# Routing of the first mixture's tokens inside the first attention

## The chip, the cores and the metric

One core of a Trainium2 chip runs the whole program, one launch. The metric is the device time in microseconds; lower is better. TensorE does the matmuls, VectorE and ScalarE the elementwise work and the reads of PSUM, GpSimd elementwise work in SBUF and indirect DMAs, SyncE issues the other DMAs.

## The reference, cut to what matters

Four layers on x of 8 sequences x 512 tokens x 256, fp32. The change touches the first and the head of the second:

```python
x = x + attn0(layernorm(x))            # 16 heads of 16, rope, causal softmax
y = layernorm(x)
logits = y @ gate_w                    # 8 experts
top_w, top_idx = top_k(logits, 2)
top_w = softmax(top_w)
x = x + sum_e combine[:, e] * (gelu(y @ w1[e] + b1[e]) @ w2[e] + b2[e])
# then a second attention with an MLP, and a mixture of 64 + 2 small experts
```

## The kernel before, in words

`attention0_phase` is one block of five instruction streams. The order of its work is written out: `ORDER` has, for each step (one pair of heads, 8 steps a sequence), the units of `STEP` (line 158), each with the number of steps that it runs ahead. `qk` turns keys and queries of a pair, `a0` to `a2` are score tiles of which VectorE takes the maxima (`a_top`), `m` turns the queries with the negated maxima in them, `b0` to `b2` are the scores again, whose exponentials ScalarE takes, `v0` to `v3` the products with the values (in even steps), `h` and `o` bring heads out and normalise them (`o` in odd steps). `BETWEEN` (line 160) hangs further units behind these: `x` turns the next sequence's normed tokens (step 0), `p0` to `p3` project its four tiles (steps 1 and 2), `t` and `y` turn and project the attention of the sequence before and add it to `g.x` (step 2), `n` norms the next sequence (step 7). Every engine follows the same order. Nearly all units share a ring of three PSUM tiles of two banks: TensorE's unit waits until the one three places back has been taken.

GpSimd puts the rope on the projected keys and queries of the next sequence and splits them (`stack_tile`, line 207: 13 operations a tile on GpSimd, or on VectorE for two tiles of the first sequence). Units `qk` of the next sequence begin in step 5 and wait for all four tiles (`stacked`). Then it adds a bias to `g.x`. VectorE also takes the statistics of the input during sequence 0. SyncE writes zeros into the 34816 rows of `sorted_x` and `sorted_y` by copying a first piece.

`route0_phase` (line 714 on) is the next block, on four groups of 8 tiles: statistics and the first guess of 1/sqrt on VectorE, three Newton steps on GpSimd (`rsqrt_refine`, line 77), normalisation into `g.y`, turning, logits by experts in three products of high and low parts, turning back, the choice of the best two experts on VectorE (15 small dependent operations, `choose`), ranks by matmuls with a triangle of ones, the rows of `sorted_x` (`place`), and 64 indirect scatters of 128 rows each by GpSimd (line 792), for which it waits at the end. Behind the last ranks VectorE makes the map of slots to experts, SyncE loads the first expert's weights and VectorE and ScalarE split them. Then comes the experts' block.

Of the kernel before, what the change touches and what calls it, by code (L numbers as in the profile page):

```python
# [88 lines left out]
def attention0_phase(nc, g, t):  # L89

    W3 = 3 * D
    with ExitStack() as ctx:
# [6 lines left out]
        def sig(name, per_turn=0):  # L99
# [21 lines left out]
        straight = sb("straight", [P, 2, H0, DH0])  # L121
# [20 lines left out]

        w_raw = probs[0][:, :, :].rearrange("p j c -> p (j c)")[:, 0:KC * W3].rearrange("p (c n) -> p c n", c=KC)
# [30 lines left out]
        RINGED = [unit for unit in ORDER if unit[0] in ("qk", "a0", "a1", "a2", "b0", "b1", "b2", "x", "p", "t", "y")]  # L174
# [4 lines left out]
        CLEARED, SPLITS = 11, 11 + 4  # L179

        BATCHES = ((0, TB), (TB, 2 * TB), (2 * TB, NT))
        steps_of = lambda batch: 2 * (batch[1] - batch[0]) + 5
        PREPARED = steps_of(BATCHES[0]) + steps_of(BATCHES[1]) + TB // 2 * 13
# [9 lines left out]
        turn_step, stacked = sig("turn_step", 11 * TB), sig("stacked", 2 * TB)  # L193
# [8 lines left out]
        attT_done, attT_hi, attT_lo = sig("attT_done", KC), sig("attT_hi", KC), sig("attT_lo", KC)  # L202
        proj_done, proj_added = sig("proj_done", TB), sig("proj_added", TB)
# [3 lines left out]
        def stack_tile(engine, n, m, turned, straight, step, done, turn):  # L207

            pairs_of = lambda ap: ap.rearrange("p h (d two) -> p h d two", two=2)
            for q in range(2):  # L210
                for e in range(2):
                    engine.tensor_tensor(pairs_of(turned[:, q])[:, :, :, e], pairs_of(qk[:, n, q])[:, :, :, 1 - e],
                                         pairs_of(unrope[:, n, q:q + 1, :])[:, :, :, e].broadcast_to([P, H0, DH0 // 2]),
                                         ALU.mult).then_inc(step.sem, step.tick())
                engine.tensor_tensor(straight[:, q], qk[:, n, q], rope[:, n, q:q + 1, :].broadcast_to([P, H0, DH0]),
                                     ALU.mult).then_inc(step.sem, step.tick())
            engine.wait_ge(step.sem, step.at(step.n, turn))
            for at in (0, DH0):
# [66 lines left out]
        def _(pool):  # L285
# [33 lines left out]
            for s in range(1, B):  # L319
# [3 lines left out]
                if s == 1:  # L323
                    refine(2)
# [2282 lines left out]
```

## Time and profile before

| | us |
|---|---|
| median of 3 runs | 2749.5 (2744.93 to 2750.41) |
| the profiled execution | 2746.9 |
| its span | 2745.2 |
| first attention's loop | about 76 to 580 |
| routing block | 580 to 709 |

The span is what the trace covers, the execution's own time lies 1.7 us above it. Starts in the trace are counted from the span's begin.

### The profile page before, as it was taken

How to read it: one execution, taken by the hardware profiler on the slowest of the kernel's cores; microseconds unless marked ns; L12 is line 12 of the kernel's file. 1: busy time of each engine (PE TensorE's matmuls, PEld its weight loads, DVE VectorE, ACT ScalarE, POOL GpSimd, SP SyncE). 2: the span in 40 equal slices, each digit the busy share in tenths (PEclk: the TensorE clock that was granted, in tenths of full speed). 3: DMA queues.
4: the chain of work that ended last, by engine and by line, in shares of the span. 5: the costliest groups of instructions: out<-in, count | busy, mean ns of one | idle time of the engine just before them, and what ended most of it. 6: DMA issues, size and time to landing. Idle time of an engine off the chain costs nothing. (4 is left out here: it accounts for less than half of the span.)

```text
span 2745.2 us, 53741 instructions
## 1 busy us (share of the span) xinstructions
PE 2419.3 (88%) x20524; PEld 2156.7 (79%) x20524; DVE 1799.5 (66%) x3223; ACT 1342.6 (49%) x2061; POOL 824.5 (30%) x1226
## 2 busy tenths in 40 slices
PE   4999999953599999935788898789999999999999
PEld 3666666632599999924677787689999999999999
DVE  7666666664488888849998888267444454544544
ACT  1555555631377777633444453344454554545454
POOL 4555566317200000055677766410000000000000
PEclk7899999976799999967899999989999999999999
DMA  9995000003477677747656565144222222222222
GB/s 302 332 334 169 2 2 2 2 6 126 156 241 238 234 230 240 220 131 181 154 148 156 152 168 147 40 138 143 91 90 86 83 89 88 86 89 87 89 78 87
DMA packets 195374, 373.31 MB, mean 136 GB/s; under 512 B 28964, under 2 KB 105960, under 8 KB 194152
## 3 DMA queue, kind: packets, MB, share of 16 engines
q1 hardware_dynamic: 185816, 343.31, 40.7%
q0 software_dynamic: 9360, 27.27, 3.0%
q8 instruction: 134, 2.20, 0.3%
q14 instruction: 64, 0.52, 0.1%
HBM read 336.95 MB, written 100.66 MB: 159 GB/s over the span
## 5 line engine op out<-in xcount | busy, mean ns | idle before, releaser
L2314 DVE TENSOR_TENSOR e_h_lo<-e_h,e_h_hi 128x512 fp32r<-128x512 f32 x320 | 222.0, 694 | 300.2 <-ACT e_h_hi L2390 300.2
L2452 PE MATMUL e_h_ps<-e_yT_hi,e_w_hi 128*128 128x256 f32 x1280 | 362.9, 283 | 3.0 <-ACT e_h L2376 2.2
L2468 PE MATMUL e_y_ps<-e_w_hi,e_h_hi 128*128 128x256 f32 x1280 | 359.1, 281 | 2.4 <-DVE e_h_lo L2314 2.3
L2452 PE MATMUL e_h_ps<-e_yT_hi,e_w_lo 128*128 128x256 f32 x1280 | 358.7, 280 | 0.0
L2452 PE MATMUL e_h_ps<-e_yT_lo,e_w_hi 128*128 128x256 f32 x1280 | 358.7, 280 | 0.0
L2468 PE MATMUL e_y_ps<-e_w_lo,e_h_hi 128*128 128x256 f32 x1280 | 355.7, 278 | 0.0
L2468 PE MATMUL e_y_ps<-e_w_hi,e_h_lo 128*128 128x256 f32 x1280 | 355.7, 278 | 0.0
L2390 ACT ACTIVATE e_h_hi<-e_h 128x512 fp32r<-128x512 f32 x320 | 202.2, 632 | 276.7 <-DVE e_h L2309 220.5
L2376 ACT ACTIVATE e_h<-e_h_ps,e_b 128x512 f32<-128x512 f32 x320 | 218.9, 684 | 175.0 <-PE e_h_ps L2452 151.3
L2309 DVE TENSOR_TENSOR e_h<-e_h,e_spread 128x512 f32<-128x512 f32 x256 | 176.8, 691 | 133.5 <-ACT e_h L2376 132.4
L462 DVE TENSOR_REDUCE a_top<-a_ring 128x2 f32<-128x1024 f32 (+3 forms) x256 | 204.2, 819 | 72.2 <-PE a_ring L651 70.8
L2452 PEld LDWEIGHTS e_h_ps<-e_yT_hi,e_w_hi 128*128 128x128 f32 x1280 | 243.7, 190 | 4.8 <-ACT e_h L2376 2.6
L2468 PEld LDWEIGHTS e_y_ps<-e_w_hi,e_h_hi 128*128 128x128 f32 x1280 | 240.9, 188 | 3.9 <-DVE e_h_lo L2314 3.3
L2452 PEld LDWEIGHTS e_h_ps<-e_yT_lo,e_w_hi 128*128 128x128 f32 x1280 | 241.7, 189 | 0.0
L2452 PEld LDWEIGHTS e_h_ps<-e_yT_hi,e_w_lo 128*128 128x128 f32 x1280 | 241.6, 189 | 0.0
L2468 PEld LDWEIGHTS e_y_ps<-e_w_lo,e_h_hi 128*128 128x128 f32 x1280 | 240.9, 188 | 0.2
L2468 PEld LDWEIGHTS e_y_ps<-e_w_hi,e_h_lo 128*128 128x128 f32 x1280 | 240.4, 188 | 0.0
L79 POOL TENSOR_TENSOR e_by_tile<-e_by_tile 128x4 f32<-128x4 f32 x24 | 8.5, 356 | 746.3 <-DVE e_by_tile L71 745.1
L517 ACT ACTIVATE a_probs<-a_ring 128x1024 f32<-128x1024 f32 (+1 forms) x192 | 168.8, 881 | 98.3 <-PE a_ring L665 97.0
L1290 PE MATMUL e_y_ps<-e_w_hi,e_h_hi 128*128 128x256 f32 x624 | 179.0, 287 | 2.9 <-DVE e_h_lo L1180 2.3
L1276 PE MATMUL e_h_ps<-e_xT_hi,e_w_hi 128*128 128x256 f32 x624 | 174.4, 280 | 1.6 <-DVE e_xT_lo L1173 1.6
L1276 PE MATMUL e_h_ps<-e_xT_hi,e_w_lo 128*128 128x256 f32 x624 | 174.2, 279 | 0.0
(371 smaller groups left out, 6772.6 us busy)
## 6 DMA issues: line engine op xcount, KB each, us to landing
e_w<-in_w SPq DMA_DIRECT2D x78, 1024.0 KB, 5.6
e_spread<-share_store SPq DMA_DIRECT2D x512, 128.0 KB, 2.8
a_keys<-rows_store SPq DMA_DIRECT2D x128, 256.0 KB, 5.0
a_queries<-rows_store SPq DMA_DIRECT2D x86, 256.0 KB, 4.9
a_running_hidden<-rows_store SPq DMA_DIRECT2D x42, 256.0 KB, 4.7
e_xs<-sorted_x SPq DMA_DIRECT2D x39, 256.0 KB, 5.1
sorted_y<-e_ys POOLq DMA_DIRECT2D x39, 256.0 KB, 5.9
e_stage_buf<-in_w_all SPq DMA_DIRECT2D x10, 512.0 KB, 3.9
```

Source lines behind the costliest of these rows:

```text
L79: pool.tensor_tensor(tmp, guess, guess, ALU.mult).then_inc(step.sem, step.tick())
L462: dve.reduce_max(top[r % 2][:, tb, :], banks(k)[:, :, at:at + (tb + 1) * P], AX.X).then_inc(top_taken.sem, top_taken.tick())
L517: act.activation(probs_of(s, r)[:, :, B_AT[i]:B_AT[i] + B_WIDTH[i]], banks(k)[:, :, 0:B_WIDTH[i]], ACT.Exp).then_inc(probs_ready.sem, prob ...
L1276: last = pe.matmul(h_ps[:, at:at + SLOT_TOKENS], l, r, start=(m == 0), stop=(m == len(ops) - 1))
L1290: last = pe.matmul(y_ps[n][:, 0:D], h_parts[a][:, f, n * P:(n + 1) * P], w2_parts[k][w][:, f, :], start=(f == 0 and m == 0), stop=(f == FC ...
L2309: dve.tensor_tensor(h[:, q % 2, :], h[:, q % 2, :], spread[r % SPREADS][:, :], ALU.mult).then_inc(scaled.sem, scaled.tick())
L2314: dve.tensor_tensor(h_parts[q % 2][1][:, :], h[:, q % 2, :], h_parts[q % 2][0][:, :], ALU.subtract).then_inc(h_lo.sem, h_lo.tick())
L2376: act.activation(h[:, q % 2, :], h_ps[q % 2][:, :], ACT.Silu, bias=b1[:, c:c + 1]).then_inc(h_ready.sem, h_ready.tick())
L2390: act.activation(h_parts[q % 2][0][:, :], h[:, q % 2, :], ACT.Copy).then_inc(h_hi.sem, h_hi.tick())
L2452: last = pe.matmul(h_ps[q % 2][:, cols], l, r, start=(m == 0), stop=(m == len(ops) - 1))
L2468: last = pe.matmul(y_ps[n][:, 0:D], h_parts[q % 2][a][:, n * P:(n + 1) * P], w2[b][:, c, :], start=(q == 0 and m == 0), stop=(q == CH - 1 ...
```

## The change

- The routing of sequence q is a set of new units in the loop, one sequence behind: `S0` statistics (step 3), `S1` scale and first guess, `S2` Newton steps (step 4), `N` normalisation (step 5), `U` turning, `L` logits, `T` turning back and `C0` first choice (step 6), `C1` second choice, `K` ranks, `W` rows (step 7). `U`, `L`, `T` and `K` take places in the ring. The last sequence's run behind the loop.
- The Newton steps are 9 VectorE operations instead of 12 on GpSimd.
- The norm `n` of sequences 3 to 7 moves from step 7 to step 3.
- The choice takes 12 operations behind the copy instead of 15, the placing 5 instead of 8.
- `stack_tile` has 8 operations over the same elements instead of 13.
- GpSimd scatters sequence q behind the stack and bias of sequence q+2, and the last two behind the loop. The normalised tokens lie in the third and fourth tile of the projected keys and queries, so VectorE waits for the scatters before it writes the third.
- SyncE spreads zeros over `sorted_x` first, then over `sorted_y` in smaller pieces, one at a time. Three more small loads and six VectorE operations for the constants stand at the start.
- The routing block keeps the map, the shares and the first weights, with two small loads; GpSimd waits for the scatters there.

```diff
         STEP = (("a0", 2), ("b0", 0), ("v0", -1), ("m", 1), ("a1", 2), ("qk", 3), ("b1", 0), ("o", -2), ("v1", -1), ("a2", 2),
                 ("v2", -1), ("b2", 0), ("v3", -1), ("h", -1))
         BETWEEN = {("b1", 0): ("x",), ("b0", 1): ("p0",), ("b1", 1): ("p1",), ("b2", 1): ("p2",), ("b0", 2): ("p3",),
-                   ("b1", 2): ("t",), ("b2", 2): ("y",), ("a2", 1): ("n",)}
+                   ("b1", 2): ("t",), ("b2", 2): ("y",), ("a2", 1): ("n",), ("a2", 5): ("n",),
+                   ("b1", 3): ("S0",), ("b0", 4): ("S1",), ("b1", 4): ("S2",), ("b1", 5): ("N",), ("b0", 6): ("U",),
+                   ("b1", 6): ("L",), ("v2", 5): ("T",), ("b2", 6): ("C0",), ("b0", 7): ("C1",), ("b1", 7): ("K",),
+                   ("o", 5): ("W",)}
         ORDER = []
         for step in range(-3, B * PAIRS + 2):
             for what, ahead in STEP:
                 s_, r_ = divmod(step + ahead, PAIRS)
                 ORDER.append((what, s_, r_))
                 for extra in BETWEEN.get((what, r_), ()):
-                    of = s_ - 1 if extra in ("t", "y") else s_ + 1
+                    of = s_ - 1 if extra[0] in "tySNULTCKW" else s_ + 1
+                    if extra == "n":
+                        of = (s_ + 1 if s_ < 2 else B) if r_ == 1 else (s_ + 2 if s_ else B)
                     if 0 <= of < B:
                         ORDER.append((extra[0], of, int(extra[1:] or 0)))
 
...
-        def stack_tile(engine, n, m, turned, straight, step, done, turn):
...
+        def stack_tile(engine, n, m, turned, step, done, turn):
+
+            pairs_of = lambda ap: ap.rearrange("p q h (d two) -> p q h d two", two=2)
+            mix = unrope[:, n].rearrange("p q (d two) -> p q d two", two=2).unsqueeze(2)
+            for e in range(2):
+                engine.tensor_tensor(pairs_of(turned[:, :])[:, :, :, :, e], pairs_of(qk[:, n])[:, :, :, :, 1 - e],
+                                     mix[:, :, :, :, e].broadcast_to([P, 2, H0, DH0 // 2]), ALU.mult).then_inc(step.sem, step.tick())
             engine.wait_ge(step.sem, step.at(step.n, turn))
+            engine.tensor_tensor(qk[:, n], qk[:, n], rope[:, n].unsqueeze(2).broadcast_to([P, 2, H0, DH0]),
+                                 ALU.mult).then_inc(step.sem, step.tick())
+            engine.wait_ge(step.sem, step.at(step.n, turn))
+            twice = lambda ap: ap.unsqueeze(2).broadcast_to([P, H0, 2, DH0])
+            engine.tensor_tensor(q_stack[m][:, n, :, 0:2 * DH0].rearrange("p h (u d) -> p h u d", u=2), twice(qk[:, n, 0]),
+                                 twice(turned[:, 0]), ALU.add).then_inc(step.sem, step.tick())
+            engine.tensor_tensor(k_stack[m][:, n, :, 0:4 * DH0].rearrange("p h (u two d) -> p h u two d", u=2, two=2)[:, :, :, 0],
+                                 twice(qk[:, n, 1]), twice(turned[:, 1]), ALU.add).then_inc(step.sem, step.tick())
+            engine.wait_ge(step.sem, step.at(step.n, turn))
+            engine.tensor_tensor(qk[:, n], qk[:, n], turned[:, :], ALU.add).then_inc(step.sem, step.tick())
...
+            def spread(name, at, size, behind):
+                dst, src = (t[rows][a:a + size, :].rearrange("(p r) d -> p (r d)", p=P)
+                            for rows, a in ((name, at), ("sorted_y", 0)))
+                sp.dma_start(dst, src).then_inc(behind.sem, behind.tick(16))
+
+            END = BLOCKS * SLOT_TOKENS
+            for at in range(0, END, TOKENS):
+                spread("sorted_x", at, min(TOKENS, END - at), zeros_spread)
+            sp.wait_ge(zeros_spread.sem, zeros_spread.at(zeros_spread.n))
+            for at in range(TOKENS, END, TOKENS // 2):
+                spread("sorted_y", at, min(TOKENS // 2, END - at), spread_zeros)
+                sp.wait_ge(spread_zeros.sem, spread_zeros.at(spread_zeros.n))
...
+            def scatter(q):
+                if q == 0:
+                    pool.wait_ge(zeros_spread.sem, ZERO_SPREADS * 16)
+                pool.wait_ge(rows_ready.sem, rows_ready.at(1, q))
+                for k in range(2):
+                    for n in range(TB):
+                        row = q * TB + n
+                        pool.indirect_dma_start(
+                            out=t["sorted_x"][:, :], out_offset=bass.IndirectOffsetOnAxis(ap=g.row[k][:, row:row + 1], axis=0),
+                            in_=y[:, n, :], in_offset=None).then_inc(written.sem, 16)
+
             prepare()
             for s in range(1, B):
+                turn_step.n = stacked.n = 0
+                for n in range(TB):
+                    stack(s, s % 2, n)
                 turn_step.close()
                 add_bias(s)
                 if s == 1:
                     refine(2)
+                else:
+                    scatter(s - 2)
+            scatter(B - 2)
+            scatter(B - 1)
...
+            def row_statistics(q):
+                y_step.n = 0
+                dve.wait_ge(proj_added.sem, proj_added.at(TB, q))
+                for n in range(TB):
+                    dve.bn_stats(y_stats[:, n, :], g.x[:, q * TB + n, :]).then_inc(y_step.sem, y_step.tick())
+
+            def row_scale(q):
+                dve.wait_ge(y_step.sem, y_step.at(TB, q))
+                dve.tensor_copy(y_half[:, 0:1], y_stats[:, 0, 0:1]).then_inc(y_step.sem, y_step.tick())
+                for n in range(TB):
+                    dve.bn_aggr(y_mv[:, n, :], y_stats[:, n, :]).then_inc(y_step.sem, y_step.tick())
+                dve.wait_ge(y_step.sem, y_step.at(2 * TB + 1, q))
+                dve.tensor_scalar(y_var[:, :], y_mv[:, :, 1], EPS, None, ALU.add).then_inc(y_step.sem, y_step.tick())
+                dve.wait_ge(y_step.sem, y_step.at(2 * TB + 2, q))
+                dve.tensor_scalar(y_half[:, :], y_var[:, :], -0.5, None, ALU.mult).then_inc(y_step.sem, y_step.tick())
+                rsqrt_seed(dve, y_step, q, y_rstd[:, :], y_var[:, :])
+
+            def row_refine(q):
+                y_refined.n = 0
+                dve.wait_ge(y_step.sem, y_step.at(2 * TB + 5, q))
+                for i in range(3):
+                    dve.tensor_tensor(y_newton[:, :], y_rstd[:, :], y_rstd[:, :], ALU.mult).then_inc(y_refined.sem,
+                            y_refined.tick())
+                    dve.wait_ge(y_refined.sem, y_refined.at(3 * i + 1, q))
...
+            def normalise(q):
+                if q + 2 < B:
+                    dve.wait_ge(stacked.sem, stacked.at(2 * TB, q + 2))
+                if q:
+                    dve.wait_ge(written.sem, written.at(0, q))
+                for n in range(TB):
+                    dve.tensor_scalar(y[:, n, :], g.x[:, q * TB + n, :], y_mv[:, n, 0:1], y_rstd[:, n:n + 1],
+                                      ALU.subtract, ALU.mult).then_inc(y_ready.sem, y_ready.tick())
+
...
+            def choose(q, k):
+                current = (logits, masked)[k]
+                best = g.best[k][:, q * TB:(q + 1) * TB]
+                dve.tensor_reduce(best, current[:, :, :], AX.X, ALU.max).then_inc(route_step.sem, route_step.tick())
+                routed()
+                dve.tensor_tensor(A[:, :, :], current[:, :, :], wide(best), ALU.is_equal).then_inc(route_step.sem, route_step.tick())
+                routed()
+                dve.tensor_tensor(A[:, :, :], ids[:, :, :], A[:, :, :], ALU.mult).then_inc(route_step.sem, route_step.tick())
+                routed()
+                dve.tensor_reduce(first[:, :], A[:, :, :], AX.X, ALU.min).then_inc(route_step.sem, route_step.tick())
+                routed()
+                dve.tensor_tensor(pick[k][:, :, :], ids[:, :, :], wide(first[:, :]), ALU.is_equal).then_inc(route_step.sem,
+                        route_step.tick())
+                routed()
+                if k == 0:
+                    dve.scalar_tensor_tensor(out=masked[:, :, :], in0=pick[0][:, :, :], scalar=-HUGE, in1=logits[:, :, :],
+                                             op0=ALU.mult, op1=ALU.add).then_inc(route_step.sem, route_step.tick())
+                    routed()
+                else:
+                    dve.tensor_tensor(both[:, :, :], pick[0][:, :, :], pick[1][:, :, :], ALU.add).then_inc(picked.sem, picked.tick())
+
+            def place_rows(q, k):
+                dve.wait_ge(ranked.sem, ranked.at(1, q))
+                dve.tensor_tensor(rank[:, :, :], ring[k][:, 0:TB * E0].rearrange("p (n e) -> p n e", n=TB),
+                                  g.head[:, :].unsqueeze(1).broadcast_to([P, TB, E0]), ALU.add).then_inc(route_step.sem,
+                                          route_step.tick())
+                routed()
...
+                dve.tensor_tensor(placed[:, :, :, :], rank[:, :, :].unsqueeze(1).broadcast_to([P, 2, TB, E0]), picks[:, :, :, :],
+                                  ALU.mult).then_inc(route_step.sem, route_step.tick())
+                routed()
+                dve.tensor_reduce(row_f[:, :, :], placed[:, :, :, :], AX.X, ALU.add).then_inc(route_step.sem, route_step.tick())
+                routed()
+                dve.tensor_copy(g.rows[:, :, q * TB:(q + 1) * TB], row_f[:, :, :]).then_inc(rows_ready.sem, rows_ready.tick())
+                dve.wait_ge(rank_taken.sem, rank_taken.at(1, q))
...
+                    if r == 2 and s >= 3:
+                        dve.wait_ge(written.sem, written.at(0, s - 2))
                     biased(s, m, r, k)
...
+            def transpose_rows(q, k):
+                pe.wait_ge(y_ready.sem, y_ready.at(TB, q))
+                for c in range(KC):
+                    for n in range(TB):
+                        last = pe.transpose(ring[k][:, c * S + n * P:c * S + (n + 1) * P], y[:, n, c * P:(c + 1) * P], g.ident[:, :])
+                    last.then_inc(yT_done.sem, yT_done.tick())
+
+            def find_logits(q, k):
+                pe.wait_ge(yT_lo.sem, yT_lo.at(KC, q))
+                split_product(ring[k][0:E0, 0:S], [((gate_hi[:, c, :], gate_lo[:, c, :]), (xnT_hi[:, c, :], xnT_lo[:, c, :]))
+                                                   for c in range(KC)]).then_inc(gates_done.sem, gates_done.tick())
+
...
+            def find_ranks(q, k):
+                pe.wait_ge(picked.sem, picked.at(1, q))
+                ranks = ring[k][:, 0:TB * E0]
+                pe.matmul(ranks, tri[:, :], both[:, :, :].rearrange("p n e -> p (n e)"), start=True, stop=False)
...
+            transpose_rows(B - 1, 2)
+            find_logits(B - 1, 0)
+            turn_logits(B - 1, 1)
+            find_ranks(B - 1, 2)
...
         @block.gpsimd
         def _(pool):
...
+            pool.wait_ge(g.written.sem, g.written.at(0, B))
...
```

## Rows read from the trace of the kernel before

**Rows 1.** Busy time by stretch: us, then busy us of PE, PEld, DVE, ACT, POOL (instructions), clock, DMA.

```profile
76.50:580.40 503.90, 489.08 (x5483) 331.51 (x5481) 323.26 (x616) 285.17 (x371) 269.28 (x404) 0.99 0.33 110
580.40:709.20 128.80, 41.31 (x240) 25.44 (x240) 65.99 (x258) 15.68 (x26) 73.53 (x112) 0.60 0.24 84
```

**Rows 2.** Timeline of POOL: start, us taken, operation, count; in brackets the idle time before.

```profile
404.78 1.00 POOL L212 TENSOR_TENSOR a_turned<-a_qk,a_unrope 128x128 f32<-128x128 f32 x2 [25.20 <-DVE a_qk L393]
...
408.19 1.42 POOL L219 TENSOR_TENSOR a_q_stack<-a_straight,a_turned 128x256 fp32r<-128x256 f32 x2
...
441.01 2.79 POOL L302 TENSOR_TENSOR x<-x,a_bias_proj 128x256 f32<-128x256 f32 x4
```

**Rows 3.** Timelines of DVE and POOL from the attention's end to the experts' start.

```profile
579.66 0.75 DVE L428 TENSOR_TENSOR x<-x,a_ring 128x256 f32<-128x256 f32 x2 [0.60 <-PE a_ring L535]
...
580.78 0.09 DVE L894 MEMSET r_three_halves<- 128x32 f32 x1 [0.37 <-PEq L92]
...
672.47 0.96 POOL L792 DMA_INDIRECT sorted_x<-y,row  x1 [0.30 <-issue]
...
673.73 1.84 POOL L792 DMA_INDIRECT sorted_x<-y,row  x1 [0.30 <-issue]
...
700.97 0.96 POOL L792 DMA_INDIRECT sorted_x<-y,row  x1 [0.30 <-issue]
...
709.19 0.20 DVE L1167 MEMSET scratch<- 128x1 f32 x6 [32.12 <-PEq L712]
```

**Rows 4.** Timelines of DVE and ACT in the routing block.

```profile
581.27 2.36 DVE L813 BATCH_NORM_STATS2 r_stats<-x 128x6 f32<-128x256 f32 x7
...
656.25 0.23 DVE L844 COPY r_logits<-r_lg_ps 128x64 f32<-128x64 f32 x1 [5.46 <-PE r_lg_ps L1023]
...
662.97 0.19 DVE L922 TENSOR_TENSOR r_apart<-r_best 128x32 f32<-128x32 f32 x1
...
666.59 0.17 DVE L952 CAST slot_expert<-r_over 1x40 int32<-1x40 f32 x1
...
673.52 1.23 DVE L964 CAST e_w_hi<-e_w 128x2048 fp32r<-128x2048 f32 x1 [5.60 <-DMA e_w<-in_w]
...
678.00 1.91 ACT L991 ACTIVATE e_w_hi<-e_w 128x2048 fp32r<-128x2048 f32 x1 [14.57 <-DMA e_w<-in_w]
```

**Rows 5.** Timeline of PE: in the loop, the last row in the routing.

```profile
397.08 1.09 PE L542 MATMUL a_ring<-ident_f,a_xn 128*128 128x128 f32 x8
...
401.93 0.39 PE L535 MATMUL a_ring<-a_w_lo,a_xnT_hi 128*128 128x512 f32 x1
...
402.16 0.39 PE L535 MATMUL a_ring<-a_w_hi,a_xnT_lo 128*128 128x512 f32 x1
...
628.80 0.34 PE L1036 MATMUL r_rank_ps<-r_both,r_ones 128*128 128x8 bf16 x8
```

**Rows 6.** Busy time by stretch, steps 3, 4 and 5 of sequence 5.

```profile
426.77:432.44 5.67, 5.58 (x74) 3.99 (x76) 4.40 (x8) 4.14 (x6) 5.51 (x8) 1.00 0.00 0
432.44:439.38 6.94, 6.94 (x92) 3.85 (x92) 4.47 (x7) 4.61 (x6) 6.86 (x11) 1.00 0.01 2
439.38:444.83 5.45, 5.18 (x66) 3.73 (x64) 4.05 (x9) 4.08 (x6) 4.26 (x7) 1.00 0.02 5
```

**Rows 7.** Timelines of DVE and POOL, small operations beside the stack.

```profile
111.77 0.66 DVE L71 TENSOR_SCALAR a_rstd<-a_rstd 128x24 int32<-128x24 int32 x1
...
438.07 0.17 DVE L468 TENSOR_SCALAR a_q_stack<-a_top 128x8 fp32r<-128x8 f32 x1
...
438.13 1.29 POOL L224 TENSOR_TENSOR a_qk<-a_straight,a_turned 128x512 f32<-128x512 f32 x1
...
438.28 1.18 DVE L471 SCALAR_TENSOR_TENSOR a_q_stack<-a_top,a_q_stack 128x8 fp32r<-128x8 f32 x1
```

**Rows 8.** Timeline of PE and busy time by stretch, in sequence 0.

```profile
115.17 0.72 PE L637 MATMUL a_pT<-a_ident_r,a_q_stack 128*128 128x128 f32 x4 [1.35 <-DVE a_q_stack L471]
...
118.00:121.00 3.00, 3.00 (x23) 2.11 (x24) 0.83 (x4) 2.05 (x2) 2.61 (x8) 0.50 1.01 328
```

More of the change, by code:

```diff
@@ L266, in _ @@
                                 const_loaded.tick(16))
+            for dst, src in ((tri_raw, t["earlier"][:, :]), (gate_raw, t["gate0"].rearrange("(c p) e -> p c e", p=P)),
+                             (ids[:, :, :], t["expert_ids"][0:TB, :].partition_broadcast(P))):
+                sp.dma_start(dst, src).then_inc(const_loaded.sem, const_loaded.tick(16))
             load_x(2)
@@ L272, in _ @@
             for at in range(0, TOKENS, step):
-                sp.dma_start(t["sorted_x"][at:at + step, :].rearrange("(n p) d -> p n d", p=P), zeros).then_inc(zeroed.sem,
+                sp.dma_start(t["sorted_y"][at:at + step, :].rearrange("(n p) d -> p n d", p=P), zeros).then_inc(zeroed.sem,
                         zeroed.tick(16))
             sp.wait_ge(zeroed.sem, zeroed.at(zeroed.n))
-            for rows, start in (("sorted_x", TOKENS), ("sorted_y", 0)):
-                for at in range(start, BLOCKS * SLOT_TOKENS, TOKENS):
-                    size = min(TOKENS, BLOCKS * SLOT_TOKENS - at)
-                    dst, src = (t[name][a:a + size, :].rearrange("(p r) d -> p (r d)", p=P)
-                                for name, a in ((rows, at), ("sorted_x", 0)))
-                    sp.dma_start(dst, src).then_inc(spread_zeros.sem, spread_zeros.tick(16))
-            sp.wait_ge(spread_zeros.sem, spread_zeros.at(spread_zeros.n))
+            def spread(name, at, size, behind):
[9 more added lines that the diff above has]
+                sp.wait_ge(spread_zeros.sem, spread_zeros.at(spread_zeros.n))
         @block.gpsimd
@@ L311, in prepare @@
                 refine(1)
-                stack(0, 0, range(TB // 2))
+                for n in range(TB // 2):
+                    stack(0, 0, n)
                 pool.wait_ge(stat_step.sem, stat_step.at(PREPARED))
@@ L444, in _ @@
                     norm(s)
+                if what == "S":
+                    (row_statistics, row_scale, row_refine)[r](s)
+                if what == "N":
+                    normalise(s)
+                if what == "U":
+                    low_rows(s, k)
+                if what == "T":
+                    take_logits(s, k)
+                if what == "C":
+                    choose(s, r)
+                if what == "K":
+                    rank_unit = k
+                if what == "W":
+                    place_rows(s, rank_unit)
                 if what == "x":
@@ L498, in high_att, with high_rows, gates_to_sbuf @@
                     act.activation(xnT_hi[:, c, :], ring[k][:, c * S:(c + 1) * S], ACT.Copy).then_inc(attT_hi.sem, attT_hi.tick())
+            def high_rows(q, k):
+                for c in range(KC):
+                    act.wait_ge(yT_done.sem, yT_done.at(c + 1, q))
+                    act.activation(xnT_hi[:, c, :], ring[k][:, c * S:(c + 1) * S], ACT.Copy).then_inc(yT_hi.sem, yT_hi.tick())
+            def gates_to_sbuf(q, k):
+                act.wait_ge(gates_done.sem, gates_done.at(1, q))
+                act.activation(by_gate, ring[k][0:E0, 0:S], ACT.Copy).then_inc(gates_out.sem, gates_out.tick())
             high_parts(0, 0)
@@ L504, in _ @@
                     high_parts(s, k)
+                if what == "U":
+                    high_rows(s, k)
+                if what == "L":
+                    gates_to_sbuf(s, k)
                 if what == "t":
```

386 lines of the change are left out of this document (121 added, 265 removed).

## The prediction

> **What bounds the kernel now.** I read the busy table by stretch first. From 76.5 to 580.4 us, the first attention's loop, TensorE is busy 489 of 503.9 us at the full clock and VectorE 323; from there to 709.2, the routing, TensorE is busy a third of the time and no compute engine is near full [rows 1]. So two stretches with two limits. In the loop GpSimd then stands 25.2 us in each sequence of 64.2 until the next sequence's first projected tile is taken [rows 2]; TensorE almost never stands. In the routing, the timeline shows the chain: the attention's last addition ends at 580.41, the next block starts 0.37 us later, GpSimd issues 64 indirect scatters at one per 1.26 us, the last ending at 701.93, and the first instruction of the experts' block stands at 709.19 [rows 3]. That stretch is 128.8 us, bound at its end by GpSimd's issue.
>
> The change moves seven eighths of this under the loop. Whether it pays is a balance: what the stretch loses against what the loop gains.
>
> **What goes and what stays behind the loop.** For the last sequence everything is still serial. Statistics of four tiles, 4 x 0.34 = 1.4 us; the normalisation of as many tiles, read and written at the same width, about as much; 32 small dependent VectorE operations (5 of the scale, 9 Newton, 1 copy, 12 choosing, 5 placing). The old ones, 24 of them, take 6.7 us from 656.25 to 662.97, 0.28 each with the ranks' matmuls between; the new ones act on half the elements, so 0.26: 8.3 us [rows 4]. The TensorE legs: turning 1.1, logits six matmuls of 512 columns at 0.23, or up to twice that at the lower clock, turning back and ranks under 1 together, with evacuations by ScalarE and a VectorE subtraction in between [rows 5]: 6 to 10, taken as 8.5. Sum 19.5. Then 8 scatters, 10.5. Then the end of the block: the only block that now ends behind scatters needs 7.3 us from the end of the last issue to the next block, the one that ends without them 0.4 [rows 3]. I take 7.3; at 0.4 the result is 7 us better. The routing block that is left: two small loads, between 1 us and the 5.6 that VectorE waits for a megabyte, taken as 3.3; the map, 662.97 to 666.76, 3.8; from there the first weights' load and their two parts, to 679.91, 13.2, as before; 0.4 to leave [rows 4]. Together 20.7. In all 19.5 + 10.5 + 7.3 + 20.7 = 58.0 instead of 128.8: **70.8 us gone**.
>
> **What the loop gains on TensorE.** Per sequence eight turns, 1.1; six matmuls with a 512-column stream whose starts lie 0.23 apart, 1.4; four turns back and eight ranks, where eight of the latter take 0.34 at the lower clock, so 0.7 at most [rows 5]. 3.2 us, on an engine with nothing to hide them: seven sequences (the eighth is in the 19.5), **22.4 us**.
>
> **What it gains on VectorE.** This decides. Call a step the work between one pair's a0 and the next one's. The new VectorE work of a sequence stands in steps 3 to 7 of the sequence behind it. Steps 3, 4, 5 are 5.67, 6.94 and 5.45 us long with VectorE busy 4.40, 4.47 and 4.05 [rows 6]: 5.1 us free. Into them go the statistics (1.35), the moved norm (1.4), scale (1.1 plus contention), Newton (9 x 0.21 = 1.9 plus contention) and the normalisation (1.35).
>
> The contention: in these steps GpSimd stacks, back to back. At 438.07 a VectorE operation of eight elements takes 0.17, the next, begun 0.15 us into a 512-element operation of GpSimd, takes 1.18, and ends as that does; at 111.77 one takes 0.66 [rows 7]. GpSimd's stack runs 36.2 us from the first taken tile (404.78 to just before 441.01), and then adds a bias for 2.8 [rows 2]. Its tiles go from 13 operations to 8 over the same elements; a 512-element one takes 1.29 and pairs of 256 take 1.42 [rows 2, 7]. With the start and the wait that each merged operation no longer has, I put this at 0.8 us a tile, so 33 us. With the step's own delays, scale begins 31 us after that first tile and Newton 35: scale is beside the stack, Newton beside the bias only. I charge scale's four small operations 1.2 and three of the nine Newton operations 0.45 each: 9.6 us in all, against 5.1 free: 4.5 over. Order costs some more, since TensorE takes a bank again only when VectorE has reduced it: laying the operations out in order I get 5.0. Seven sequences, less 1.4 in the two that have no norm to move: **33.6**. If the ring of three banks hid what is over, it would be 1 a sequence; if nothing fell into the gaps, 9.6.
>
> Steps 6 and 7 and the start of the next: 1.3 subtracting, 0.25, 1.55 and 1.55 choosing, 1.2 placing. TensorE itself lengthens them by 3.2 and the norm leaves step 7; the budget closes, but in step 7 the ranks wait for the reduction behind the second choice and the next a2 stands behind the placing: 0 to 2.7 a sequence, taken as 1, in six: **6**. TensorE's waits for the stack, 0.3 a sequence, go: -2.
>
> A warning that this isn't absorbed stands in the same trace. In sequence 0 VectorE has the input's statistics in each step and the seed in step 4, and TensorE waits 1.35 us for the negated maxima at 115.17, a wait that it hardly has later [rows 8].
>
> GpSimd's 8 scatters a sequence, 10.1, fit into its 25.2 us wait; they are released in step 7 and end about 2 us ahead of the next first tile. Before the third tile is written VectorE waits for them; by my layout they have landed 3 us earlier. The zeros: the copies into sorted_x (8.5 of 16 times 4.2 MB) now go first; the DMA stretch that ran from 39 to about 240 us puts their end near 150, and the first scatter is due near 200. The slower ones into sorted_y behind them delay nobody. Six more small operations at the start stand against ten fewer of the stack: nothing.
>
> The sum: -70.8 + 22.4 + 33.6 + 6 - 2 = -11 us. The profiled execution took 2746.9 (span 2745.2); -11 gives 2736; the median of the runs is 2.6 above it, **2738 us**.
>
> The Trainium skill ("SBUF — State Buffer", Who interferes with whom) states that a VectorE operation with two inputs in SBUF, or one in a two-port mode, and a GpSimd operation reading SBUF lock each other out for a whole instruction. The 1.18 us at 438.28 agree. By that rule each Newton operation that meets the stack would wait for one GpSimd operation; the sum above charges this for three of nine only.
>
> **Rivals.**
> 1. The ring and the gaps hide VectorE's work. For it: 323 of 504 us busy. Against: sequence 0. Then 1 us a sequence is left over: -70.8 + 22.4 + 7 - 2 = -43, **2706 us**.
> 2. Slower: VectorE's dependent chain is caught by GpSimd's stack. The chain is 13 operations long and each lets GpSimd begin another one between. It decides at one point: whether the stack still runs when Newton begins (33 against 35 us after the first tile, so 2 us of margin; broadcast operands of three dimensions or VectorE's interruptions can use them up). At 0.66 an operation this costs 2.7 a sequence more, 19; at the length of the merged operations, about 1.1, 8.8 a sequence, 61; taken as 30. Beside it: around that wait of 1.35 us the granted clock fell to 0.50, the lower level of 1.2 GHz, for some 10 us, and a step of 5.5 us took some 2 longer [rows 8]; seven times 14. -11 + 30 + 14 = +33, **2780 us**.
> 3. The scatters land too late for the third tile: in the routing an issue beside VectorE's cast of the weights took 1.84 us instead of 0.96 [rows 3]. Eight such put them 2 to 3 us behind in five sequences: **2751 us**.
>
> **How the numbers follow.** The layout as above has 43 in 100; its own range 2720 to 2756 (bounds 5 us on the 70.8, 12 on what is over). Rival 1 20, rival 2 29, rival 3 8. What a measurement can't tell from no change is 0.2%, 2744 to 2755. Faster: 20 + 31 of the first = 51; same: 11 + 4 = 15; slower: 29 + 4 + 1 = 34. The range goes to the middles of rivals 1 and 2 and a little past the latter: 2706 to 2788.
>
> **What would show it.** Right: the stretch from the last sequence's addition to the experts' first instruction is 58 us; the indirect scatters stand in eight groups of eight; a sequence of the loop goes from 64 to some 73 us; TensorE's longest waits in the loop are for the reductions (a_top) in steps 3 to 5 and at the ranks. Wrong: Newton's operations at 0.6 us and more (rival 2), a granted clock of 0.5 in the loop (rival 2), waits for the scatters on VectorE (rival 3), a sequence of 68 us (rival 1), or a block end behind the scatters that is far from 7 us.

## The result

The changed kernel takes 2778.4 us (median of 4 runs, 2770.5 to 2782.5), the kernel before 2747.9 (4 runs): a ratio of 1.0104, 95% interval 1.0081 to 1.0127. It is slower by 1.0%; the forecast was 2738 us. The profiled execution spans 2780.6 us, 35.4 more than that of before.

The profile after, first by stretch. The first row is one whole sequence of the loop, from one bias of GpSimd to the next; the second is a part of it. The third is another whole sequence, the first of the five that have a wait of 4.0 us, cut at a matmul instead of a bias; the fourth reaches from the last sequence's addition to the experts' first instruction (columns as in [rows 1]).

```profile
337.78:419.70 81.92, 75.28 (x744) 50.07 (x743) 55.31 (x124) 39.09 (x51) 43.45 (x44) 0.88 0.04 14
337.80:357.20 19.40, 19.40 (x148) 11.78 (x147) 13.53 (x34) 9.62 (x12) 2.77 (x4) 0.50 0.00 1
137.80:213.80 76.00, 68.88 (x746) 46.34 (x742) 55.13 (x123) 38.66 (x52) 38.80 (x39) 0.98 0.74 264
683.77:736.78 53.01, 6.95 (x30) 4.26 (x30) 17.86 (x67) 3.92 (x5) 7.68 (x8) 0.52 0.18 61
```

The same stretch of one sequence in the kernel before:

```profile
376.77:441.01 64.24, 63.47 (x714) 43.30 (x713) 42.35 (x78) 36.99 (x49) 38.10 (x56) 1.00 0.01 2
```

The fourth row answers to [rows 1]: 128.8 us have become 53.0, 75.8 gone. But the last addition now ends at 683.8 and not at 580.4: the loop has grown by 103.4. The 7.8 us that are left lie behind 736.78, where both kernels run the same instructions; in another unchanged rest (the kernel before with a new stack, below) they took 7.2 us more than in the profile of before too, so they are variation between executions.

The sequence of the first row grew by 17.7 us, and the rows divide them. TensorE is busy 75.28 us instead of 63.47, but at a mean clock of 0.88. Experiment 12 below has the same work, and one of its sequences, cut at the same matmuls, runs at 1.00 throughout: there it is busy 67.07. So 3.6 us are added work and 8.2 us the same work at the lower clock. Its idle time went from 0.77 to 6.64 us: 5.9. Together 17.7. Four of the five sequences with such a wait are like this one, 81.8 to 81.9 us. The other one, in the third row, has the wait of 4.0 us too, but the low clock for 3.4 us only: it took 76.0 us, 5.9 less, with 7.1 of them idle.

TensorE's waits in five sequences of the changed kernel (us in total, times, longest), and what stands around one of the longest, in the timelines of PE, DVE and POOL:

```profile
PE a_ring L872 <- DVE a_top L633: 20.0, 5, 4.0
PE a_ring L901 <- DVE a_top L633: 5.8, 11, 0.6
PE a_ring L788 <- DVE a_top L633: 4.2, 5, 0.8
```

```profile
419.48 0.75 PE L872 MATMUL a_ring<-a_ident_r,a_k_stack 128*128 128x128 f32 x4 [4.04 <-DVE a_top L633]
...
410.00 1.39 DVE L489 BATCH_NORM_STATS2 a_y_stats<-x 128x6 f32<-128x256 f32 x4
...
412.86 1.20 DVE L642 SCALAR_TENSOR_TENSOR a_q_stack<-a_top,a_q_stack 128x8 fp32r<-128x8 f32 x1
413.98 4.31 DVE L441 TENSOR_SCALAR a_xn<-x,a_mv,a_rstd 128x256 f32<-128x256 f32 x4
418.21 1.21 DVE L633 TENSOR_REDUCE a_top<-a_ring 128x2 f32<-128x1024 f32 x1
...
419.80 0.66 DVE L497 TENSOR_SCALAR a_y_var<-a_y_mv 128x4 f32<-128x4 f32 x1
...
423.08 0.15 DVE L506 TENSOR_TENSOR a_y_newton<-a_y_rstd 128x4 f32<-128x4 f32 x1
...
414.11 1.41 POOL L246 TENSOR_TENSOR a_q_stack<-a_qk,a_turned 128x512 fp32r<-128x512 f32 x1
415.48 1.32 POOL L248 TENSOR_TENSOR a_k_stack<-a_qk,a_turned 128x512 fp32r<-128x512 f32 x1
416.88 1.26 POOL L251 TENSOR_TENSOR a_qk<-a_qk,a_turned 128x512 f32<-128x512 f32 x1
```

The reader is to see three things. The norm that was moved to step 3 (L441, four operations) takes 4.31 us; in its old place, where GpSimd stood, it took 1.38. Its first operation took 0.40 us and the other three 1.36 to 1.42, about as long as GpSimd's beside them. (The row statistics, L489, beside the same stack, were not slowed: 1.39 us for four, and 1.41 behind the loop with GpSimd idle.) TensorE waits 4.04 us for the reduction queued behind the norm, and from 419.1 on, still in that wait, the granted clock is 0.50, its lower level of 1.2 GHz, for 20.5 us. Newton's nine operations, over which my forecast worried, run at 0.15 to 0.16 us here and in all sequences but one: stack and bias were over. In the one at 583 us, which has no moved norm in front of it, they come earlier, and four of them take 0.65 beside the bias.

The end of the stretch, in the timelines of POOL and DVE:

```profile
702.97 0.96 POOL L359 DMA_INDIRECT sorted_x<-a_qk,rows  x1 [19.88 <-DVE rows L576]
...
711.83 0.96 POOL L359 DMA_INDIRECT sorted_x<-a_qk,rows  x1 [0.30 <-issue]
...
718.40 0.19 DVE L997 TENSOR_TENSOR r_apart<-best 128x32 f32<-128x32 f32 x1 [15.70 <-PEq L92]
...
736.78 0.20 DVE L1172 MEMSET scratch<- 128x1 f32 x6 [1.55 <-PEq L957]
```

### The profile page after: what moved, and what is told of

Read it like the earlier page. It is cut to its first block and busy times, and to the rows that moved or that the text cites. A ratio compares the mean times of both kernels' runs of the same rounds, so it can differ in the third digit from the quotient of the medians.

```text
span 2780.6 us, 53710 instructions
## 1 busy us (share of the span) xinstructions
PE 2461.6 (89%) x20524; PEld 2183.6 (79%) x20524; DVE 1838.8 (66%) x3352; ACT 1345.3 (48%) x2061; POOL 798.2 (29%) x1028
## 5 line engine op out<-in xcount | busy, mean ns | idle before, releaser
L2473 PE MATMUL e_y_ps<-e_w_hi,e_h_lo 128*128 128x256 f32 x1280 | 355.4, 278 | 0.0
L1295 PE MATMUL e_y_ps<-e_w_hi,e_h_lo 128*128 128x256 f32 x624 | 175.1, 281 | 0.0
```

Of the source, the lines that this page charges most:

```text
L1295: last = pe.matmul(y_ps[n][:, 0:D], h_parts[a][:, f, n * P:(n + 1) * P], w2_parts[k][w][:, f, :], start=(f == 0 and m == 0), stop=(f == FC ...
L2473: last = pe.matmul(y_ps[n][:, 0:D], h_parts[q % 2][a][:, n * P:(n + 1) * P], w2[b][:, c, :], start=(q == 0 and m == 0), stop=(q == CH - 1 ...
```

## The experiments

Theory A: VectorE's operations are caught by GpSimd's stack, TensorE waits in one piece for what is queued behind them, and its clock falls at such a wait. Theory B: the loop has more work than fits, wherever it stands, and the place of an operation is worth nothing. The kernel before took 2750 to 2751 us in the groups of runs of the first eight experiments and of those labelled 12 to 15, but 2757 to 2759 in the other three groups; compare ratios there.

**1. The norm put back**

```
-  ("a2", 1): ("n",), ("a2", 5): ("n",),
+  ("a2", 1): ("n",),
-  if extra == "n":
-      of = (s_ + 1 if s_ < 2 else B) if r_ == 1 else (s_ + 2 if s_ else B)
```

> The changed kernel with one edit undone: the norm of the next sequence (four VectorE operations) stands again just ahead of that sequence, where GpSimd stands idle, and not in step 3. Theory A (the moved norm is caught by GpSimd's stack; VectorE is 3 us late, TensorE waits 4.0 us and its clock is then 0.50 for 20.5 us, in five sequences): the four operations take 1.4 us again and not 4.3, the wait of 4.0 us and the low clock go, a sequence falls from 81.9 us to about 68, and the time by 5 x 14 less some 5: 2713 us. Theory B (VectorE simply has more work in steps 3 to 5 than fits, whatever it is): 1.4 us a sequence back, 2771 us, and the clock still falls. Theory C (the choice of the experts fills step 7 now, and the norm beside it makes TensorE wait there): 2778 us or more, with the wait at the ranks grown.

Measured: 2773.3 us, ratio 1.008 (1.0058 to 1.0103). The wait of 4.0 us is gone and the norm takes 1.41 us, but the sequences only fall to 78 to 80 us. DVE and PE:

```profile
332.83 1.09 DVE L495 TENSOR_SCALAR a_y_var<-a_y_mv 128x4 f32<-128x4 f32 x1
...
334.03 1.25 DVE L69 TENSOR_SCALAR a_y_rstd<-a_y_var 128x4 int32<-128x4 int32 x1
...
336.92 0.66 DVE L507 TENSOR_TENSOR a_y_newton<-a_y_newton,a_y_half 128x4 f32<-128x4 f32 x1
...
367.18 1.41 DVE L439 TENSOR_SCALAR a_xn<-x,a_mv,a_rstd 128x256 f32<-128x256 f32 x4
...
336.87 0.39 PE L885 MATMUL a_ring<-a_kq_T 64*128 64x256 f32 x2 [1.82 <-DVE a_top L631]
...
341.19 0.50 PE L899 MATMUL a_ring<-a_qT_max,a_kq_T 64*128 64x512 f32 x2 [1.98 <-DVE a_top L631]
```

With 3 us less in front of them scale and Newton come earlier, and now they are caught, scale by the stack (1.09, 1.25), Newton by the bias behind it (0.65 four times). The waits are 1.8 us in each sequence, and here another of 2.0, instead of one of 4.0, and the clock still falls, to a mean of 0.87 to 0.93 in a sequence. Theory A's price for this edit was wrong, and so was its ground: it took the norm for the only victim.

**2 to 4. One part alone**

In the kernel before, the norm in step 3 (the edit of 1, the other way round):

> The kernel before with this one edit alone: the norm of the sequence after the next stands in step 3, as in the changed kernel; nothing of the routing is moved. Theory A: the four operations take about 4.3 us instead of 1.4 and TensorE waits 2.5 to 3 us for the reduction behind them in five sequences. If such a wait is enough for the clock to fall, +13 x 5 = 65 us, 2813; if it is not, since the statistics of the rows aren't in the same step, +2.5 x 5 = 12, 2760. Theory B (load, not place): the same operations in the same number, so within 3 us of 2748.

In the changed kernel, TensorE's turns repeated to fill its wait:

```
+  again = 8 if r == 5 and 1 <= s <= 5 else 1
-  for n in range(TB):
+  for n in list(range(TB)) * again:
```

> The changed kernel; TensorE repeats the four turns of the negated maxima of pair 5 seven times more (3.8 us at the full clock) in sequences 1 to 5, just ahead of the instruction that waited 4.0 us, so that it has work in that gap; VectorE and GpSimd are as they were. Theory A (the wait is what drops the clock): the granted clock stays 1.00, the scale operations still take 4.3 us, and a sequence falls from 81.9 to about 72 us: 5 x 10 less, 2728 us. If the clock falls for another reason: 2778 us or up to 20 more.

In the kernel before, the stack of 8 operations:

> The kernel before with the stack of 8 operations a tile instead of 13, nothing else. Both theories: GpSimd needs 8.6 us a tile instead of 9.05 and then waits 1.7 us longer in each sequence, since it is not what sets the loop: 2748 us, within 4. If the longer operations lock VectorE out for longer each time, up to 1 us in each of six steps, +20: 2768 us.

Measured: the norm alone 2761.2 us, 1.0027 (1.0016 to 1.0039); the wait filled 2762.3, 1.0054 (1.0034 to 1.0074); the new stack alone 2747.5, 0.999 (0.998 to 1.0). The second is the clearest: TensorE has 19 us more to do, VectorE and GpSimd are as they were, and the kernel is 16 us faster. One sequence of it, and the rows of the norm and of the wait:

```profile
331.84:407.82 75.98, 71.19 (x773) 48.84 (x772) 54.85 (x125) 38.66 (x51) 43.46 (x44) 0.98 0.05 15
```

```profile
402.07 4.34 DVE L441 TENSOR_SCALAR a_xn<-x,a_mv,a_rstd 128x256 f32<-128x256 f32 x4
...
407.60 0.54 PE L872 MATMUL a_ring<-a_ident_r,a_k_stack 128*128 128x128 f32 x4 [1.67 <-DVE a_top L633]
```

The norm is caught as before, the wait is 1.67 us, and the clock is 0.98. So the long fall follows TensorE's standing still. The time is still 34 us above the 2728 that theory A gave: TensorE stays idle for 4.8 us in this sequence.

**5 to 8. Where scale, Newton and the bias stand**, all on top of 1.

```
5: -  ("b0", 4): ("S1",), ("b1", 4): ("S2",)
   +  ("b2", 4): ("S1",), ("b0", 5): ("S2",)
6: 5, and GpSimd's add_bias(s) ahead of the stack of s
7: 1, and add_bias(s) ahead of the stack of s
8: 7, and Newton of sequences 0 to 6 on GpSimd behind its stack
```

> On top of the kernel with the norm put back (2773 us, 78 us a sequence, in which the operations of scale and Newton took up to 1.25 us beside GpSimd's stack and bias): scale's operations one half step later, behind step 4's last reduction, and Newton's behind step 5's first one, so that the stack is over when Newton begins. Theory A (what is lost is small VectorE operations caught by GpSimd, TensorE's waits behind them and the clock that falls at such a wait): Newton at 0.16 us each, about 3 us less of VectorE time a sequence, the waits of 1.8 and 2.0 us in steps 4 and 5 gone, the clock at 1.00 nearly throughout, 70 us a sequence: 2773 - 6 x 8 = 2725 us. Theory B (it is the amount of VectorE and TensorE work, wherever it stands): within 5 us of 2773.

> The same, and GpSimd's additions of the bias stand ahead of the stack and not behind it, so that GpSimd is idle from the stack's end on and catches nothing of scale or Newton. Theory A: 1 to 1.5 us a sequence less than with the scale moved alone, 2718 us. If the bias beside step 0 catches as much there, or delays the stack's start: equal to it or up to 6 us more.

> On top of the kernel with the norm put back: only GpSimd's bias moved ahead of the stack; scale and Newton stand where the changed kernel has them. Theory A: the stack now ends about when Newton begins, so that Newton runs at 0.16 us each (2 us less a sequence) while scale is still caught: 74 us a sequence, 2750 us. Theory B: 2773 us within 5.

> On top of the kernel with the bias ahead of the stack: Newton's steps of sequences 0 to 6 run on GpSimd, between its stack and its scatters, as 12 operations of some 0.4 us; VectorE has nine operations less a sequence. Theory A: VectorE gains what Newton takes there (1.8 us, and whatever it was caught for), GpSimd has the time (it waits over 30 us for the rows), so 1.5 to 2 us a sequence below the kernel with the bias first alone: 2738 us. If the normalisation then has to wait for GpSimd (a chain of 12 operations takes 7 us or more), the rows come later and TensorE waits at the turns of the rows: as much as the kernel with the bias first alone or more.

Measured: 2759.6 us, 1.004 (1.0022 to 1.0058); 2753.5, 1.0013 (0.9992 to 1.0033); 2772.1, 1.008 (1.0063 to 1.0097); 2773.2, 1.0094 (1.0077 to 1.0111). A half step later and a bias earlier give back 20 us with the same operations, so their place counts, and B, as stated, is out. But theory A's 2725 and 2718 for 5 and 6 were 35 us too low, and 7 and 8 missed. Scale, not Newton, is what holds the reduction there; in 8, with Newton gone from VectorE altogether, it takes what it took, and TensorE waits as long:

```profile
411.46 1.08 DVE L502 TENSOR_SCALAR a_y_var<-a_y_mv 128x4 f32<-128x4 f32 x1
...
412.65 1.25 DVE L69 TENSOR_SCALAR a_y_rstd<-a_y_var 128x4 int32<-128x4 int32 x1
...
415.49 0.53 PE L894 MATMUL a_ring<-a_kq_T 64*128 64x256 f32 x2 [1.83 <-DVE a_top L640]
...
415.45 0.20 POOL L79 TENSOR_TENSOR a_y_newton<-a_y_rstd 128x4 f32<-128x4 f32 x1
```

Moving Newton to VectorE, an item of the change, is worth nothing either way at this place.

**9 to 11.** 9 is 6 with the statistics and the normalisation in two halves each, on either side of a reduction. 10 is the kernel before with the edits of 2 and of 4 together. 11 is the changed kernel with the edits of 5 and 6 but its norm in step 3.

> On top of the kernel with scale and Newton later and the bias first (2753 us; 73.6 us a sequence, TensorE waiting 0.5, 0.5, 0.7 and 1.3 us in steps 3 to 5 and 1.8 in step 7): the row statistics and the normalisation are split into two halves of two tiles, one ahead and one behind step 3's and step 5's last reduction. Theory A (TensorE waits where VectorE has more than some 1.2 us between two reductions): the 0.5 of step 3 and half of the 1.3 of step 5 go, 1 us a sequence, 2746 us. If the sum of VectorE's work in the step decides: the waits move to the next reduction and the time stays at 2753 us within 3.

> The kernel before with both edits that were tried on it one at a time: the stack of 8 operations and the norm in step 3; nothing of the routing moved. Alone the norm in step 3 cost 11 us, its four operations taking 2.5 us beside the old stack; the new stack alone nothing. Theory A (each norm operation waits for one GpSimd operation, and those are longer now): about 4.3 us for the four, as in the changed kernel, TensorE waits 2 us or more for the reduction behind them; 2775 us, and 2800 if the clock falls with it in each of the five sequences. If the length of GpSimd's operations doesn't matter: 2761 us.

> The changed kernel with its norm where it put it (step 3), but scale and Newton later and the bias first, as in the kernel of 2753 us: the two differ by the place of the norm alone. Theory A: the four operations take 4.3 us again in five sequences, TensorE waits over 2 us behind them; 2.9 us a sequence without a fall of the clock, 13 with it: 2768 to 2818 us, and 2785 as the middle. Theory B (amount of work): within 5 us of 2753.

Measured: 2800.8 us, 1.0167 (1.0143 to 1.0191); 2813.2, 1.0206 (1.0191 to 1.0222); 2818.6, 1.0224 (1.0208 to 1.0239). 9 contradicts A and 11 is dearer than it should be; both show stalls of another kind (last section), so they were run again. 10 has no scatters in its loop and no such stalls, and it is the find of this group. The norm and GpSimd beside it in 2 (old stack), then in 10 (new stack) with TensorE's wait:

```profile
378.08 2.47 DVE L382 TENSOR_SCALAR a_xn<-x,a_mv,a_rstd 128x256 f32<-128x256 f32 x4
...
378.56 0.78 POOL L217 TENSOR_TENSOR a_straight<-a_qk,a_rope 128x256 f32<-128x256 f32 x1
```

```profile
382.48 5.37 DVE L381 TENSOR_SCALAR a_xn<-x,a_mv,a_rstd 128x256 f32<-128x256 f32 x4
...
389.03 0.75 PE L632 MATMUL a_ring<-a_ident_r,a_k_stack 128*128 128x128 f32 x4 [4.42 <-DVE a_top L463]
```

Four operations of the same size take 0.62 us each beside GpSimd's pieces of 0.5 to 0.78, and 1.34 beside pieces of 1.3. Trace against trace, the norm alone ends the loop 20 us later, the stack alone 3 us earlier, and both together 32 us later (last addition at 611.9 instead of 579.7), though no routing stands in it. So the merged stack, harmless by itself, more than doubles what one catch costs. The 32 us are not all that the median shows: the profiled execution is the fastest of its five, 2788.5 us, the routing block in it took 8 us more than in the profile of before, and what the other executions have on top stays open.

**12 to 15.** The kernels of 6, 9 and 11, and the changed kernel itself, on one chip.

> The kernel with the norm back, scale and Newton later and the bias first, once more, on the same chip as the next three. If the stalls of ScalarE and TensorE's instruction issue beside GpSimd's scatters (3.1 and 3.3 us in each sequence of the smoothed kernel, none in this kernel's first run) belong to the chip and the moment: they can show here too, and the time is then above 2753, up to 2790 us, and the smoothed kernel is within 10 us of it. If they belong to the smoothed kernel: 2753 us without them.

> The smoothed kernel again, beside the one it is to be compared with. Chip theory: within 8 us of it, 5 us better if the halves fill the gaps. Kernel theory: 2800 us and the stalls beside the scatters in each sequence.

> The changed kernel with scale and Newton later and the bias first, its norm in step 3, again beside the kernel that differs from it in the norm's place alone. Theory A: 15 to 65 us above that kernel, whichever chip it is; the four norm operations take over 4 us and TensorE waits 4 us behind them five times.

> The changed kernel itself on the same chip: 2778 us if this chip is as the first; on one where ScalarE stalls beside the scatters 10 to 40 us more, since it has six such groups of scatters in the loop.

Measured: 2750.7 us, 1.0002 (0.9985 to 1.002); 2756.0, 1.0049 (1.0015 to 1.0084); 2779.5, 1.0113 (1.0091 to 1.0134); 2779.9, 1.0125 (1.0095 to 1.0155). The first and the third differ by the norm's place alone: 29 us. The third and the fourth differ by the place of scale, Newton and the bias alone: nothing, though in experiments 1 to 6, with the norm back, that place was worth 20. Norm and scale must both leave the stack; moving one of them leaves most of the loss. One sequence of the first, and the norm, the wait and one sequence in the third:

```profile
366.07:438.62 72.55, 67.07 (x746) 45.65 (x743) 51.93 (x123) 38.54 (x52) 42.50 (x44) 1.00 0.04 15
```

```profile
418.12 5.35 DVE L441 TENSOR_SCALAR a_xn<-x,a_mv,a_rstd 128x256 f32<-128x256 f32 x4
...
424.65 0.75 PE L872 MATMUL a_ring<-a_ident_r,a_k_stack 128*128 128x128 f32 x4 [4.70 <-DVE a_top L633]
```

```profile
381.98:460.85 78.87, 69.58 (x746) 46.76 (x742) 54.31 (x123) 38.64 (x52) 43.24 (x45) 0.96 0.04 15
```

In the first TensorE is idle for 72.55 - 67.07 = 5.5 us a sequence, hardly less than the 6.6 of the changed kernel. But no piece is above 1.3 us, and the clock is 1.00 here and 0.90 to 0.98 in the four sequences around it, against 0.88 in four of the changed kernel's five and 0.98 in the other. In the third the clock shows only half of the loss: over five sequences it takes 28.0 us more than the first, 14.4 of them idle time of TensorE and 13.7 longer busy time for the same matmuls. Smoothing the pieces further (13) was no gain.

**16 to 18. A version below both?** On top of 6, ScalarE normalises the finished rows of sequences 0 to 6 (16, and again as 18), and the next sequence's rows too (17).

```
+  act.activation(y[:, n, :], g.x[:, q * TB + n, :], ACT.Identity, bias=y_newton[:, n:n + 1],
+                 scale=y_rstd[:, n:n + 1])
```

> On top of the kernel with the norm back, scale and Newton later and the bias first (2751 us): the normalisation of the finished rows (sequences 0 to 6) runs on ScalarE as four scaled copies with a bias; VectorE has 1.37 us less in step 5 and one small operation more. Theory A (what is left of the loss is VectorE's excess in steps 3 to 7, one for one): TensorE's wait of 1.3 us in step 5 and part of the 0.7 before it go, 1.5 to 2 us a sequence: 2739 us, below both kernels. Rival: four operations of some 0.45 us in ScalarE's queue hold up the exponentials of step 5, TensorE waits for a_probs there instead: 2751 us or more.

> The same, and the norm of the next sequence (1.4 us of VectorE in step 7) on ScalarE too. Theory A: the waits of 0.6 and 0.3 us in step 7 shrink, another 0.8 us a sequence: 2733 us. Rival: the turns of the next sequence's rows wait for ScalarE, and the exponentials behind it: no better than the one with the finished rows alone, or up to 10 us worse.

> The kernel with the finished rows' normalisation on ScalarE once more. In its first run ScalarE stalled 3.1 and 3.3 us beside the scatters of each sequence, and the kernel before took 2759 us there and not 2750. Without these stalls theory A gives 1.6 us a sequence less than the kernel of 2751 us (TensorE's waits for the reductions were 16 us in five sequences in the first run, 24 in that kernel's), 2740 us, 0.996 of the kernel before. If the stalls come with this kernel, they are there again and the time is 2780 us.

Measured: 2781.5 us, 1.0084 (1.0069 to 1.0099); 2787.0, 1.01 (1.0083 to 1.0116); 2781.8, 1.0083 (1.0069 to 1.0096). The waits for reductions fell as forecast, from 24 us in five sequences to 16, but ScalarE stalls beside the scatters in all three profiles (last section). What such stalls cost, two other kernels show, each once with them and once without: the loop ends 44 us later in 9 than in 13, and 39 later in 11 than in 14. In 16 it ends 34 later than in 12, so the stalls are enough for that, and the rival, ScalarE's longer queue, is neither shown nor ruled out. No version below both kernels was found. Whether 16 is one without those stalls is open.

## Why the prediction was wrong

- **The stretch behind the loop: right.** 53.0 us against 58.0. Its terms: up to the first scatter 19.2 (19.5 forecast), eight scatters 9.8 (10.5), the block's end 5.6 (7.3), the routing block 18.4 (20.7).
- **TensorE's added work: nearly right.** 3.2 us a sequence were forecast; 3.6 are measured. One term was too small: turning back the logits, put with the ranks at 0.7 at most, takes 1.05 and the ranks 0.35. Seven times 0.4 is 3 us.
- **The waits: right in sum, by luck.** "4.5 over", laid out as 5.0, and 1 more at steps 6 and 7, less the 0.3 that go, is 5.7 a sequence; 5.9 are measured. Their parts were not right. "The moved norm (1.4)" stands among the work without any contention and measured 4.31; Newton's 1.35 of contention measured nothing in six of seven sequences. In the sum the 1.4 us of the two sequences without a norm are taken off once and not twice, a slip of 1.4 us.
- **The step that failed: the sum charges the waits at their own length and leaves the clock out.** The fall to 0.50 was seen, in [rows 8], behind a wait of 1.35 us, and was put into rival 2 alone. It costs 8.2 us in each of four sequences. Behind them two more stretches at 0.50, 13.7 and 10.2 us long, cost some 10 at the same rate, an estimate. With the 3 us of added work these are some 45; between the 60 that I summed for the loop and the 103.4 measured lie 43.
- **Why it fell: the moved norm, and behind it scale.** The norm was the one large group of operations whose cover is taken away by the move, from where GpSimd stands to where it stacks. The row for it was in the argument, 1.18 us for an operation begun beside one of GpSimd's [rows 7], and I applied it to small operations only. Shown by 12 against 14 (29 us) and, outside the changed kernel, by 10. But the norm is not the only cause: with it back and scale left beside the stack (1), the waits of 1.8 us that are left let the clock fall again, and the ratio only goes from 1.0104 to 1.008. Either alone is enough for most of the loss. With both cured (12) the loop still ends 75 us later than before, 15 above the 60 of the sum, and what is gained behind it is used up.
- **The merged stack was booked as a gain** (33 us instead of 36.2; measured 34.5). That it lengthens each catch was missed.
- **Rival 2 named 2780 us, and the measured time is 2778**: right in kind (VectorE caught, clock falls), wrong in place, and the nearness is luck. Newton was caught in one of seven sequences of the changed kernel; that it can be in six, 1 showed. **Rival 3** did not come: no wait of VectorE for the scatters stands in the trace; GpSimd waits 32 us a sequence for the rows. **Rival 1**, that the gaps hide VectorE's work, is out.
- The Trainium skill ("SBUF — State Buffer", Who interferes with whom) has whichever of VectorE and GpSimd issues second wait for the other's whole instruction, where VectorE's has two inputs in SBUF or is in a two-port mode. The norm's operations have one large input, so the rule reaches them only in that mode, which no trace shows. The 0.62 against 1.34 us in 2 and 10 agree with it. Applied to the norm with the 1.18 us of [rows 7] it would have given 4.7 us instead of 1.4, an estimate.

## What to carry to other kernels

When work is moved, ask of each piece of it, also the one that only makes room, what the other engines do at its new place; beside a GpSimd that doesn't pause the norm's operations lasted as long as GpSimd's, while the row statistics did not. Merging small operations on one engine made each catch of the other longer. Read TensorE's waits by their longest piece and not only by their sum: 5.5 us a sequence in pieces up to 1.3 left the clock between 0.90 and 1.00, 6.6 with one of 4.0 brought it to 0.88 in four sequences of five. But a sequence of 14 with a wait of 4.7 kept 0.96 and lost by 9.3 us of idle time instead, so the sum counts too. And undo suspects together, not only one by one: norm and scale each hid what the other cost.

## What was not expected of the hardware

- **How long the clock stays low varies.** Behind the five waits of 4.0 us it was 0.50 for 3.4 us once and 20.5 four times in the first profile of the changed kernel, and for 17.1, 3.4, 17.1, 17.1 and 3.4 us in the second (experiment 15). In 7, behind waits of 1.8 to 1.9 us, it was 13.7 us in each of six sequences; in 3, with waits of 1.7, no stretch at 0.50 in these sequences is longer than 6.8.
- **Newton's twelve small operations on GpSimd** (8) come every 0.28 us and take 0.20 each; VectorE's nine (7) come every 0.20 us and take 0.16.
- **ScalarE stalls beside scatters, in some runs.** In 9, 11, 16, 17 and 18 ScalarE waits 3 us and more, up to 4.7, once or twice in a sequence while GpSimd issues its eight scatters, though the work that it needs is done, and TensorE's instructions come late by up to 1.9 us. In 18, the timelines of PE, ACT and POOL:

```profile
449.94 0.51 PE L880 MATMUL a_ring<-a_ident_r,a_q_stack 128*128 128x128 f32 x4
...
454.12 1.02 ACT L711 ACTIVATE a_kq_T<-a_ring 128x1024 fp32r<-128x1024 f32 x1 [4.65 <-remote]
...
451.91 0.96 POOL L357 DMA_INDIRECT sorted_x<-a_qk,rows  x1 [0.30 <-issue]
```

The turn ends at 450.45 and its copy starts at 454.12. In the profiles of 1, 3, 5 to 8 and 12 to 15, with the same scatters, there is none of it. Kernel 9 showed it once and, as 13, once not, so it is not the kernel's alone; nor is it the chip's, since the record gives the same chip for 1 to 4 as for 16 and 17. The three groups that show it are those in which the kernel before took 2757 to 2759 us and not 2750. What causes it stays open.
